# Expert lists of a routed feed-forward block: down projection over the full array, filler matmuls, earlier table reads, last sums in pieces

## What is computed

```python
sc = sigmoid(x @ gate_weight.T) + gate_bias          # 32 experts in 4 groups
topidx = top 6 of the experts of the 2 best groups
routed = sum over the 6 of weight * (silu(x @ w_gate[e]) * (x @ w_up[e])) @ w_down[e]     # hidden 128
shared = silu(x @ shared_w_gate) * (x @ shared_w_up) @ shared_w_down                      # hidden 128
lg = topidx[:, 0] // 2                                                                   # one of 16 anchors
anchor = (silu(x @ anchor_w_gate[lg]) * (x @ anchor_w_up[lg])) @ anchor_w_down[lg]        # hidden 64
out = routed + shared + 0.1 * anchor
```

## Time and profile before

| | us |
|---|---|
| Median of 3 runs | 455.22 |
| The three runs | 455.22, 457.03, 452.00 |
| Profiled execution, whole | 450.88 |
| Profiled execution, span of its instructions | 448.9 |

### The profile page before, as it was taken

How to read it: one execution, slowest core, us unless ns; L and a number is a source line. 1 busy time by engine, 2 the same in 40 slices (tenths; PEclk the granted TensorE clock), 3 DMA queues, 4 the chain that set the end, 5 groups by cost and what they waited for, 6 DMA issues and landing times.

```text
span 448.9 us, 9872 instructions
## 1 busy us (share of the span) xinstructions
PE 368.5 (82%) x2504; PEld 300.2 (67%) x2505; DVE 264.6 (59%) x1126; ACT 189.7 (42%) x534; POOL 267.0 (59%) x188
## 2 busy tenths in 40 slices
PE   6999999898999696358999999899999999992000
PEld 4786879696878575225679878788888888881000
DVE  0565889898888867934444455455555555551523
ACT  1150351535353333001127667666776667661000
POOL 5000003888478888876007777687778677778860
PEclk9999999999999859565559999999999999997555
DMA  8999999877695439945227899799899888987977
GB/s 231 320 319 311 331 407 323 190 168 145 150 373 155 90 88 310 311 105 116 70 54 130 149 148 155 130 159 151 154 149 154 152 147 159 157 141 138 245 132 225
DMA packets 66115, 84.66 MB, mean 189 GB/s; under 512 B 16456, under 2 KB 60518, under 8 KB 65606
## 3 DMA queue, kind: packets, MB, share of 16 engines
q1 hardware_dynamic: 37702, 61.09, 47.1%
q0 software_dynamic: 27520, 22.49, 32.6%
q10 hardware_dynamic: 864, 0.73, 0.5%
HBM read 45.00 MB, written 39.14 MB: 187 GB/s over the span
## 4 chain that ended last, share of the span: by engine, by line
POOL 27%; DMA 22%; PE 21%; issue 16%; DVE 6%; ACT 5%; ACTq 1%; POOLq 1%; SPq 1%; DVEq 0%
DMA sums_d<-e_sb,tok 16%; POOL rows_d L428 16%; POOL sums_d L450 7%; PE B L476 6%; POOL sums_d L460 4%; PE B L776 3%; DMA e_sb<-rows_d 2%; PE B L790 2%; PE B L511 2%; ACT e_sb L962 2%; DMA rows_d<-xrow,slot 1%; PE B L560 1%; PE B L764 1%; ACTq L300 1%; ACT UPW L938 1%
## 5 line engine op out<-in xcount | busy, mean ns | idle before, releaser
L450 POOL DMA_INDIRECT sums_d<-e_sb,tok x87 | 135.2, 1554 | 66.3 <-ACT e_sb L962 43.4
L428 POOL DMA_INDIRECT rows_d<-xrow,slot x77 | 104.8, 1361 | 98.3 <-issue 97.9
L776 PEld LDWEIGHTS B<-e_sb,UPW 128*128 128x128 f32 x796 | 107.1, 200 | 21.4 <-issue 11.4
L776 PE MATMUL B<-e_sb,UPW 128*128 128x128 f32 x796 | 117.6, 290 | 0.3 <-DVE e_sb L1435 0.2
L790 PE MATMUL B<-W,e_sb 128*128 (+1 forms) x224 | 78.2, 432 | 3.6 <-issue 1.1
L1435 DVE COPY e_sb<-B 128x256 f32<-128x256 f32 x112 | 47.6, 425 | 49.2 <-issue 27.6
L938 ACT COPY UPW<-W 128x512 f32 (+1 forms) x112 | 63.0, 563 | 5.1 <-DVE table L1414 5.1
L949 ACT ACTIVATE e_sb<-B 128x128 f32<-128x128 f32 (+1 forms) x112 | 30.8, 275 | 57.1 <-PE B L776 52.6
L1462 DVE TENSOR_TENSOR e_sb<-e_sb,B 128x128 f32<-128x128 f32 (+1 forms) x112 | 32.2, 288 | 36.9 <-ACT e_sb L949 35.7
L764 PE MATMUL B<-ident,e_sb 128*128 128x128 f32 x224 | 46.5, 293 | 7.0 <-DMA e_sb<-rows_d 7.0
L790 PEld LDWEIGHTS B<-W,e_sb 128*128 128x128 f32 (+1 forms) x224 | 35.5, 199 | 16.7 <-issue 15.7
(11 more groups left out here) (204 smaller groups left out, 478.3 us busy)
## 6 DMA issues: line engine op xcount, KB each, us to landing
e_sb<-rows_d SPq DMA_DIRECT2D x112, 145.0 KB
rows_d<-padrow SPq DMA_DIRECT2D x1, 6960.0 KB, 31.5
W<-in_wx SPq DMA_DIRECT2D x1, 6643.0 KB, 33.3
sums_d<-padrow SPq DMA_DIRECT2D x4, 1440.0 KB, 33.7
W<-in_wx SPq DMA_DIRECT2D x10, 516.5 KB, 9.6
W<-in_wx SPq DMA_DIRECT2D x1, 4576.0 KB
W<-in_pt SPq DMA_DIRECT2D x4, 666.0 KB, 6.9
W<-sums_d SPq DMA_DIRECT2D x2, 1232.0 KB, 9.9
```

The lines of the kernel that those rows point to most:

```text
L428: pool.indirect_dma_start(rows_d, bass.IndirectOffsetOnAxis(ap=slot[0:n, t, j:j + 1], axis=0), xrow[0:n, t, :], None).then_inc(done, 16)
L450: pool.indirect_dma_start(sums_d[c], bass.IndirectOffsetOnAxis(ap=tok[:, c:c + 1], axis=0), Y[:, c, :], None, compute_op=ALU.add).then_inc ...
L776: mm = pe.matmul(B[2 + u % 2][:, m * P:(m + 1) * P], UPW[:, u % 2, at:at + P], GT[:, u % 2, k, :], start=k == 0, stop=k == KC - 1)
```

## The change

Four parts. First, anchor tiles write their hidden values to a buffer of their own, `H_anchor` (it lies on `edges`, whose last use is over by then). It is set to zero once; the anchor's hidden values fill the upper 64 partitions, and the down product runs over all 128. The weights there are zero too, so the result is the same. Second, ten `stay_busy` products of 128 by 256 follow `shared_down(5)`, into bank 5. Third, the table reads move ahead: on TensorE the read for `down(i-1)` goes ahead of `up(i)` and its waits; on VectorE the reads for `take_rows(i+2)` and `accumulate(i-1)` go ahead of the wait for the silu of tile i. Fourth, the first three of the last sums are loaded and added in four pieces each, instead of one, one and two.

```diff
-PIECES = [[(0, NT)], [(0, NT)], [(0, 6), (6, NT)], [(0, 4), (4, 7), (7, 9), (9, 10), (10, NT)]]
+PIECES = [[(0, 3), (3, 6), (6, 9), (9, NT)]] * 3 + [[(0, 4), (4, 7), (7, 9), (9, 10), (10, NT)]]
...
+        H_anchor = edges
...
             shared_down(5)
+            stay_busy(10, 5, w_sgu)
 
             pe.wait_ge(ld["lists"], 16)
...
-            def down(i, u):
-                anchor = is_anchor(u)
-                size, at = (ANCHOR_WX, ANCHOR_UP_COLS) if anchor else (WX, UP_COLS)
-                e = entry(mybir.EngineType.PE, 0, i, (ANCHOR_COLS if anchor else W_COLS) - size)
-
+            def down_weights(i, u):
+                size, at = (ANCHOR_WX, ANCHOR_UP_COLS) if is_anchor(u) else (WX, UP_COLS)
+                e = entry(mybir.EngineType.PE, 0, i, (ANCHOR_COLS if is_anchor(u) else W_COLS) - size)
+                return W[:, bass.ds(e, size)][:, at:at + D]
+
+            def down(i, u, weights):
...
                 pe.wait_ge(H_ok, i + 1)
-                n = ANCHOR_HIDDEN if anchor else HIDDEN
-                pe.matmul(B[6 + u % 2][:, 0:D], H[0:n, u % 2, :], W[0:n, bass.ds(e, size)][:, at:at + D],
-                          start=True, stop=True).then_inc(D_ps, 1)
+                hid = H_anchor if is_anchor(u) else H
+                pe.matmul(B[6 + u % 2][:, 0:D], hid[:, u % 2, :], weights, start=True, stop=True).then_inc(D_ps, 1)
 
             def list_tile(i, u, j):
+                behind = j is not None or i >= 1
+                if behind:
+                    weights = down_weights(i - 1, u - 1)
                 up(i, u)
...
-                    down(i - 1, u - 1)
+                    down(i - 1, u - 1, weights)
...
             step(dve.tensor_tensor(valid[:, :], edges[:, 1, :], edges[:, 0, :], ALU.subtract))
+            dve.memset(H_anchor[:, :, :], 0.0)
             dve.wait_ge(table_ok, 1)
...
-            def take_rows(i, v):
-
+            def columns(i, v):
                 at = entry(mybir.EngineType.DVE, 2, i, ALPHA_COL)
+                return at, ring[:, bass.ds(place_of(i) + D, 1)] if is_anchor(v) else None
+
+            def take_rows(i, v, cols):
+
+                at, token = cols
                 mask = valid[:, bass.ds(i, 1)]
-                if is_anchor(v):
-                    token = ring[:, bass.ds(place_of(i) + D, 1)]
...
-            def accumulate(i, v, j):
-
-                total = ring[:, bass.ds(place_of(i), D)]
+            def sum_tile(i):
+                return ring[:, bass.ds(place_of(i), D)]
+
+            def accumulate(i, v, j, total):
+
...
             def hidden(i, u, j):
+                ahead = j is not None or i + 2 < XT
+                if ahead:
+                    cols = columns(i + 2, u + 2)
+                if is_anchor(u - 1):
+                    total = sum_tile(i - 1)
                 dve.wait_ge(silu_ok, i + 1)
...
-                dve.tensor_tensor(H[0:n, u % 2, :], S[0:n, u % 2, :], ups, ALU.mult).then_inc(H_ok, 1)
+                out = H_anchor if is_anchor(u) else H
+                dve.tensor_tensor(out[0:n, u % 2, :], S[0:n, u % 2, :], ups, ALU.mult).then_inc(H_ok, 1)
```

More of the change, by code:

```diff
@@ L788, in down @@
                 pe.wait_ge(H_ok, i + 1)
-                n = ANCHOR_HIDDEN if anchor else HIDDEN
-                pe.matmul(B[6 + u % 2][:, 0:D], H[0:n, u % 2, :], W[0:n, bass.ds(e, size)][:, at:at + D],
-                          start=True, stop=True).then_inc(D_ps, 1)
+                hid = H_anchor if is_anchor(u) else H
+                pe.matmul(B[6 + u % 2][:, 0:D], hid[:, u % 2, :], weights, start=True, stop=True).then_inc(D_ps, 1)
             def list_tile(i, u, j):
+                behind = j is not None or i >= 1
+                if behind:
+                    weights = down_weights(i - 1, u - 1)
                 up(i, u)
-                if not isinstance(i, int) or i + 2 < XT:
+                if j is not None or i + 2 < XT:
                     turn_rows(i + 2, u + 2)
-                if not isinstance(i, int) or i >= 1:
-                    down(i - 1, u - 1)
+                if behind:
+                    down(i - 1, u - 1, weights)
             turn_rows(0, 0)
@@ L802, in _ @@
             groups(pe, list_tile)
-            down(XT - 1, XT - 1)
+            down(XT - 1, XT - 1, down_weights(XT - 1, XT - 1))
         @block.scalar
@@ L1461, in hidden @@
                     ups = B[2 + u % 2][:, P:2 * P]
-                dve.tensor_tensor(H[0:n, u % 2, :], S[0:n, u % 2, :], ups, ALU.mult).then_inc(H_ok, 1)
+                out = H_anchor if is_anchor(u) else H
+                dve.tensor_tensor(out[0:n, u % 2, :], S[0:n, u % 2, :], ups, ALU.mult).then_inc(H_ok, 1)
                 if is_anchor(u - 1):
-                    accumulate(i - 1, u - 1, j)
-                if j is not None or i + 2 < XT:
-                    take_rows(i + 2, u + 2)
+                    accumulate(i - 1, u - 1, j, total)
+                if ahead:
+                    take_rows(i + 2, u + 2, cols)
             dve.wait_ge(ring_ok, 1)
-            take_rows(0, 0)
-            take_rows(1, 1)
+            take_rows(0, 0, columns(0, 0))
+            take_rows(1, 1, columns(1, 1))
             groups(dve, hidden)
```

## The result

The changed kernel takes 435.86 us (median of 4 runs, 434.94 to 436.99). The kernel before, with one more run, takes 453.61 us (451.86 to 457.03). The execution profiled after is the longest of its four, 436.99 us, with a span of 435.0.

The account below looks back on a forecast made before the run. No engine bounds the whole: TensorE at the low clock holds the head, GpSimd paces afterwards, then GpSimd and DMA the end. Terms 8.5 + 0 + 2.5 = 11.0 off 455.2 gave 444.2 us, range 438 to 451.

Parts of the forecast that it names:

- mostly one bubble per anchor tile: Routed stage: GpSimd additions 2.01 us apart against 1.86 at fastest, lost mostly to a bubble at each anchor tile.
- The head: Anchor tiles at the list stage's start: wide downs and fillers, one term, gain 8.5 us, ends 3.5 and 10.4.
- I leave it where it is: Head: tile 5's transposes wait until 213.35 for a row load of 6.23 us, taken as unchanged.
- the forecast's case with the clock high throughout: Head, from tile 5's transposes to tile 9's down end: 11.7 us at the high clock, a gain of 10.4.
- the case that I chose: Same stretch of the head: clock low for about two more tiles, then high; 13.5 us, a gain of 8.6.
- The fillers: Ten products before the head, 4.3 us in a 4.72 us gap: cost nothing, keep the clock up at 202.
- Value 0: Table reads moved ahead of the waits, routed stage and head: only slack, 0 gained, bounds 0 to 1 us.
- The pieces: Ring additions at the end: first three last sums in pieces, gain 2.5 us, ends 5.0 and -3.4.
- Clock low: Rival: the clock stays low through the head, gain 6.0, 449.2 us; chance 0.17.
- width nothing: Rival: wide downs do nothing in the head and the clock stays low, gain 2.5, 452.7 us; chance 0.08.
- row loads in TensorE's place: Rival: row loads of tiles 6 to 9 limit the head, 3 to 5 off 8.5, about 448.5 us; chance 0.10.
- the slower one: Rival: a table read ahead of the product delays each routed tile, 15 us lost against 11 gained, 459 us; chance 0.03.

Follow-up runs that it names:

- b1: Changed kernel with the four chains given out by the routed tile's number, loop body of 24 tiles; 430.31 us, ratio 0.943 to before.
- b2: Changed kernel with the loop body of 24 tiles and three turns, chains as they were; 431.57 us, ratio 0.960 to before.
- a1: Changed kernel without the ten filler products; 436.26 us, ratio 0.958 to the kernel before.
- e2: Kernel before with the ten filler products alone; 454.25 us, ratio 1.005 to before.
- e3: Kernel before with the table reads moved ahead of the waits alone; 448.93 us, ratio 0.986 to before.
- a3: Changed kernel with the table reads back where they were; 441.67 us, ratio 0.972 to the kernel before.
- c1: Changed kernel with TensorE's table read alone back behind the transposes, VectorE's still ahead; 434.50 us, ratio 0.967 to before.
- job 1: The job, on one chip, that held the four kernels with one part alone added to the kernel before; kernel before there 454.15 us, 19 runs.
- e1: Kernel before with the anchor tiles' down product over 128 partitions alone; 447.72 us, ratio 0.985 to before.
- a2: Changed kernel with the anchor downs back at 64 partitions; 447.63 us, ratio 0.983 to the kernel before.

## Why the prediction was wrong, point by point

**What bounds the kernel: right.** The additions on GpSimd pace the stage, and the round of additions makes the bubble: b1, which alters the round (and the body, which b2 shows to be worth nothing), gained 5.4 us there. But "mostly one bubble per anchor tile" claims too much for it: 4.4 us above the fastest pace are left in b1. "No TensorE or VectorE time is in it" was true of the one round that I read and not of all.

**The head: right mechanism, term too small.** The width carries it: 8 to 11 us of head are saved whenever the downs are wide (23.9 to 25.8 in seven profiles) and never when they are narrow (33.8 to 35.0 in seven). In all seven wide profiles the clock is back within 11 us of tile 0's transposes (in a1 and b2 it falls once more for a few microseconds), in all seven narrow ones only 32 to 36 us behind them, at the first routed tiles. How the gain divides between the stalls and the clock was not isolated. My 8.5 rested on the step "I leave it where it is": tile 5's transposes were to stay at 213.35 behind their row load, with two anchor tiles at the low clock behind them. In the changed kernel they came at 214.91 although tile 0 had come 2.7 us later, and the clock was back at 212, before them. From there to the end of tile 9's down it took 12.4 us; the forecast's case with the clock high throughout had 11.7, the case that I chose 13.5. The pace of 1.6 us for an anchor tile at the high clock measured 1.67, and the 2.14 at the low clock 2.13 in b1. That first addition at 228.79, where 228.3 was forecast, is a coincidence of a later start and a shorter head. Against the runs as a group the term is 9.9 us: a mean of 34.4 narrow, 24.5 wide.

**The fillers: right that they cost nothing, wrong in sharing the term.** They run from 195.27 to 199.75 us and the clock stays high to 204.6, but TensorE still idles for 4.90 us behind them, the clock falls as tile 0 starts, and e2 and a1 show no time gained.

**The table reads: the step that failed.** "Value 0", with bounds of 0 to 1 us, measured about 3 us in the 86 steps: 1.6 to 3.2 on the first chip (e3), 3.1 to 4.4 on the second (a3), 2.0 to 3.1 on the third (c1 against the kernel before, with the other parts). The means are 172.5 with the reads behind the waits (seven profiles) and 169.3 with them ahead (six, without b1). The claim was that VectorE was not on the path, since the rows of one round showed none of it. The view of what ended each engine's waiting shows how full the time around that round was. Groups of VectorE in 236 to 400 us of the kernel before, then in 236 to 395 us of the changed one, then in 236 to 400 us of e3, which has the moved reads alone (the number behind the second bar is the idle time ahead and what ended it):

```profile
L1435 DVE COPY e_sb<-B 128x256 f32<-128x256 f32 x96 | 40.8, 425 | 37.5 <-issue 24.3 <-PE B L764 5.6 <-PE B L776 5.4
L1462 DVE TENSOR_TENSOR e_sb<-e_sb,B 128x128 f32<-128x128 f32 x82 | 23.5, 287 | 28.6 <-ACT e_sb L949 28.1
```

```profile
L1443 DVE COPY e_sb<-B 128x256 f32<-128x256 f32 x94 | 39.3, 418 | 0.5
L1478 DVE TENSOR_TENSOR e_sb<-e_sb,B 128x128 f32<-128x128 f32 x79 | 22.7, 288 | 65.0 <-ACT e_sb L954 63.9 <-issue 0.4
```

```profile
L1441 DVE COPY e_sb<-B 128x256 f32<-128x256 f32 x97 | 40.6, 419 | 0.5
L1475 DVE TENSOR_TENSOR e_sb<-e_sb,B 128x128 f32<-128x128 f32 x82 | 23.6, 288 | 65.7 <-ACT e_sb L953 53.8 <-issue 11.9
```

The idle time ahead of the PSUM copy went from 37.5 us to 0.5, in e3 as in the changed kernel, and now lies ahead of the product, where VectorE waits for ScalarE. The copy releases the next tile's up, hence its silu, and ScalarE can't weigh one tile until it has done the silu of the next. GpSimd shows the gain as fewer long steps: with the reads behind the waits 26 to 34 of the 86 are over 1.9 us (seven profiles), with them ahead 20 to 27 (six). That the copy, the up and the silu are the way by which it gets there is read from the order of the instructions; no run isolated it. The row loads, which wait for the metadata that VectorE takes behind the copy, are another way that stays open.

**The pieces: right, 0.5 short.** Twelve pieces were to cost the ring 2.3 us in place of 5.0. The ring took 18.1 to 19.0 us in pieces and 21.0 to 22.3 whole, means of 18.5 and 21.5, a gain of 3.0 where I took 2.5. At its fastest it is nine steps of 1.86, 16.7 us, so the pieces still cost 1.8. The price of a piece was too low: 3.09 x 3 / 11 = 0.84 leaves out what each sum costs however short it is, and a piece of 768 columns took 0.96 (last section).

**The sum and its base.** The terms were 8.5 + 0 + 2.5 = 11.0. Measured by stretches they are 9.9 + 3 + 3.0 = 16, and 17.7 us separate the two medians. The miss of 8.3 us divides so: 4.9 are the terms (3 the reads, 1.4 the head, 0.5 the pieces), and 1.6 are the base, since the kernel before came out at 453.61 in place of 455.22. The other 1.8 I can't apportion. Medians of a few runs leave that much open: the kernel before spread by 5 us in its first four runs and by 14 in job 1 (446.26 to 460.22, 19 runs). The start of the list stage, which no part was meant to change, moves by more than that from profile to profile; in the two profiles above it took 2.7 us off the gain. My range allowed nothing to be gained on the reads beyond 1 us, and so ended too high: without the 3 us of the reads the result would have been about 439, inside it.

**The rivals.** Clock low (449.2), width nothing (452.7), row loads in TensorE's place (448.5) and the slower one (459) all fell. Of the third its sign was seen once, in a1's wait of 1.04 us for rows, but not its price. The Trainium skill's rule on which weight loads are pulled ahead (TensorE: Matmul & The Clock Gate, Part 2: What happens when you issue a matmul) names two cases, row groups that don't conflict and a load into the background weight buffer. By the first, the only one that the prediction drew on, the width would have been worthless. Rows 4 and e1 speak against that here: the loader idled 0.65 us behind a down over half the rows and not at all behind one over all of them.

## What to carry to other kernels

When one engine paces a stage with bubbles, read many of its waits before you call another engine's time slack: one round without VectorE in it did not show that 0.3 us per tile on VectorE was worth nothing. Where a matmul uses half the rows between matmuls that use all, try padding it with zeros, by the weight loads behind it and by the granted clock. Give buffers out by a count of the items that use them, not by the number of the tile, when some tiles use none. Profile the kernel before more than once before a time is derived from one execution's start times.

## What the runs showed of the hardware

- TensorE's granted clock did not follow the busy time of its records. With narrow downs 31.3 busy us of 33 (e2) and 24.9 of 25 (a2) stayed at 0.50; with wide ones the clock came back to 1.00 after a stretch of 4.73 us busy in 6.3. The columns, the passes and the types of the records were the same; the down over 128 rows in place of 64, and the closer packing that goes with it, were the difference, and no run tells the two apart. In the changed kernel only one wide down, at 210.21, lay in that stretch. Zeros in half the rows did not hinder it.
- An addition that GpSimd issues while VectorE adds two SBUF operands is held up, and VectorE is not. In the kernel before, the addition at 419.52 ended 1.42 us behind VectorE's sum. In the changed kernel the four that started inside a piece ended 1.43 behind it (404.84 + 1.98 = 406.82, the piece 404.43 + 0.96 = 405.39). The piece at 403.25 started inside the ring addition of 402.98 to 404.53 and took 0.96 like the others. Lines of VectorE in the changed kernel, the last of them behind GpSimd's end (421.14):

```profile
403.25 0.96 DVE L1497 TENSOR_TENSOR h<-h,W 112x768 f32<-112x768 f32 x1 [7.39 <-DMA W<-sums_d]
404.43 0.96 DVE L1497 TENSOR_TENSOR h<-h,W 112x768 f32<-112x768 f32 x1 [0.23 <-DMA W<-sums_d]
...
412.16 0.69 DVE L1497 TENSOR_TENSOR h<-h,W 112x512 f32<-112x512 f32 x1 [0.39 <-DMA W<-sums_d]
...
427.57 1.23 DVE L1497 TENSOR_TENSOR h<-h,W 112x1024 f32<-112x1024 f32 x1 [9.83 <-DMA W<-sums_d]
```

- Sums of 512, 768 and 1024 columns took 0.69, 0.96 and 1.23 us, and 2816 took 3.09. That is 0.27 per 256 columns and about 0.15 for each sum, with and without GpSimd at work.
